# An adaptive-norm feed-forward kernel: a second home for x, one group turned instead of summed on TensorE, another load order, and a wait for GpSimd

## The chip, the cores and the metric

The kernel runs on one core of a Trainium2 chip. The metric is the device time of one execution in microseconds (us); lower is better. Each time given for a kernel is the median of several executions.

## The reference

x has 32 batches of 64 rows of 512 values, cond 32 rows of 256. In float32:

```
q_emb = relu(cond @ W3 + b3)                       # (32, 512)
x1    = (64 * x + sum of x over the 64 rows) * q_emb[:, None, :]
h0    = relu(x1 @ W2 + b2)                         # (32, 64, 512)
w1    = ternary(W_fc)                              # (2048, 512)
y     = square(relu(h0 @ w1.T))                    # (32, 64, 2048)
yn    = y * rsqrt(mean(y * y, last) + 2**-23)
out   = x + yn @ ternary(W_proj).T                 # W_proj (512, 2048)
```

ternary(w) takes groups of 64 weights; scale is the mean of their absolute values, and each weight becomes -scale, 0 or +scale (round and clip of w / scale, in bfloat16).

## The kernel before

The 2048 rows of x make 4 groups of 512 rows (8 batches each), a group 4 tiles of 128 rows (t). The hidden size 2048 makes 16 tiles (j) of 128.

**Stage one, 16 units** (unit u: group g = u // 4, column block m = u % 4). For a group, sum_x multiplies every 128x128 block of x by the constant matrix sum_mat (64 times the row itself plus the batch's sum, so it transposes x and does the sum in the same product) into PSUM ps_out[:, k]; for each of the 4 blocks k, DVE's scale_x multiplies by q_t from PSUM into x1_t[:, g % 2, k] (a ring of two groups). make_h0(u) then is 4 float32 products of 128x512. ACT's relu_h0(u) applies bias and relu into h0_f (ring of 2), DVE's round_h0(u) rounds to h0_hi, and GpSimd's rest_of_h0(u) subtracts to get h0_lo (both float32r parts that TensorE multiplies in one pass each). sum_x(0) stands before unit 0, sum_x(g + 1) before unit 4g + 2 (SUMS_AT = 2). Three PSUM buffers (ACC_RING) hold products, so unit u waits for relu_h0(u - 3).

**Weights, 16 pairs, beside it.** A pair is 128 x 1024 weights. SyncE's queue loads it (load_pair, three raw buffers), ACT takes the absolute value and the sign (read_pair), DVE sums groups of 64 and makes the scale (sum_pair), ACT spreads the scale (spread_pair), DVE makes the ternary weights with three tensor_tensor operations (ternary_pair), SyncE's queue transposes by DMA (turn_pair), ACT copies into w_t (keep_pair). step(i) of ACT is keep(i - 2), read(i + 2), spread(i + 1); step(i) of DVE is sum(i + 1), ternary(i). STEP_AT_UNIT and STEP_AT_TILE say at which unit or tile each step stands; every engine works strictly in the order written:

```
STEP_AT_UNIT = {0: 0, 1: 1, 3: 2, 4: 3, 5: 4, 7: 5, 8: 6, 9: 7, 11: 8, 12: 9, 13: 10, 15: 11}
STEP_AT_TILE = {1: 12, 3: 13, 5: 14, 7: 15}
```

In DVE's loop over units, unit u is: round_h0(u - 1), then at u % 4 == 2 the four scale_x of the next group, then its step. In ACT's loop it is relu_h0(u - 1), then its step.

**Stage two, 64 tiles** (tile v: group v // 16, hidden tile j = v % 16). hidden(v) is 8 float32r products into ps_acc, ACT takes relu, square (y) and square again (y_sq, ring of 2), DVE's split_y(v) makes y_hi (cast) and y_lo (subtraction), project(v) is 8 products into ps_out. TensorE's order is hidden(v + 2), project(v). add_squares(v) adds y_sq into sq_acc on GpSimd (the last one on DVE); at the end of a group DVE's sum_parts reduces it, one small product finishes the sum, inverse_root and finish scale ps_out, add x and store.

**SyncE's queue** issues all loads of x, W2 (load_wv) and the pairs in one written order, with waits in it. x of every group goes to one buffer x_sb, so load_x(g) waits until all of group g - 1 has been summed (xt_done); what stands behind it in the queue waits as well. At the end x_sb takes x again for the residual (load_res).

Of the kernel before, what the change touches and what calls it, by code (L numbers as in the profile page):

```python
# [12 lines left out]
P = 128  # L13
# [15 lines left out]
def wait(engine, semaphore, count):  # L29
    if count > 0:  # L30
        engine.wait_ge(semaphore, count)


def adaln_ffn(
# [44 lines left out]
    SUMS_AT = 2  # L79
    STEP_AT_UNIT = {0: 0, 1: 1, 3: 2, 4: 3, 5: 4, 7: 5, 8: 6, 9: 7, 11: 8, 12: 9, 13: 10, 15: 11}  # L80
    STEP_AT_TILE = {1: 12, 3: 13, 5: 14, 7: 15}
    KEEP_AT_TILE = {8: 14, 9: 15}

    x_rows = x.rearrange("b n d -> (b n) d").rearrange("(g t p) d -> g p t d", p=P, t=TT)
    out_rows = out.rearrange("b n d -> (b n) d").rearrange("(g t p) d -> g t p d", p=P, t=TT)

    with ExitStack() as ctx:
        def sb(name, shape, dt):
            return ctx.enter_context(nc.sbuf_tensor(name, shape, dt))
# [4 lines left out]
        def sem(name):  # L94
            return ctx.enter_context(nc.semaphore(name))
# [18 lines left out]
        sum_mat = sb("sum_mat", [P, P], F32)  # L114
        ident_f = sb("ident_f", [P, P], F32)
# [24 lines left out]
        ps_out = psum("ps_out", [P, TT, BANK], F32)  # L140
# [13 lines left out]
        x_loaded = sem("x_loaded")  # L154
# [28 lines left out]
        split = sem("split")  # L183
# [30 lines left out]
        def _(sp):  # L214
            def load_pair(i):
                wait(sp, sign_ready, i - RAW_RING + 1)
                sp.dma_start(raw[:, i % RAW_RING, :].rearrange("p (i w) -> p i w", i=2), PAIRS[i][0]
                             ).then_inc(raw_loaded[i % RAW_RING], 16)

            def turn_pair(i):  # L220
                sp.wait_ge(tern_ready, i + 1)
                wait(sp, wt_ready, i)
                sp.dma_start_transpose(out=w_turned[:], in_=w_tern[:, i % RING, :]).then_inc(turned, 16)

            def load_wv(i):
                cols = slice(i * P, (i + 1) * P)
                sp.dma_start(wv_sb[:, :, cols], w_v[:, cols].rearrange("(k p) d -> p k d", p=P)
                             ).then_inc(wv_loaded[i], 16)

            def load_x(g):  # L230
                sp.wait_ge(xt_done, KD * g)
                sp.dma_start(x_sb[:], x_rows[g]).then_inc(x_loaded, 16)
# [12 lines left out]
            load_pair(0)  # L245
            load_wv(1)
            load_pair(1)
            load_wv(2)
            load_x(1)
            load_wv(3)  # L250
            load_pair(2)
            load_pair(3)
            for i in range(len(PAIRS)):
                if i + RAW_RING + 1 < len(PAIRS):
                    load_pair(i + RAW_RING + 1)
                turn_pair(i)
                if i == 1:
                    load_x(2)
                if i == 4:
# [12 lines left out]
        def _(pe):  # L272
            def sum_x_block(t, k):
                return pe.matmul(ps_out[:, k, t * P:(t + 1) * P], x_sb[:, t, k * P:(k + 1) * P], sum_mat[:],  # L274
                                 start=True, stop=True)

            def sum_x(g):
                pe.wait_ge(x_loaded, 16 * g)
                pe.wait_ge(x1_ready, KD * g)
                for k in range(KD):  # L280
                    for t in range(TT):
                        last = sum_x_block(t, k)
                    last.then_inc(xt_done, 1)
# [88 lines left out]
            for t in range(TT):  # L372
                if t == TT // 2:
                    pe.wait_ge(condt_ready, 1)
                    pe.wait_ge(wq_loaded, 16)
                    for m in range(KD):
                        for k in range(KQ):
                            last = pe.matmul(ps_x[:, m * BATCHES:(m + 1) * BATCHES], wq_sb[:, k, m * P:(m + 1) * P],  # L378
                                             cond_t[:, k, :], start=(k == 0), stop=(k == KQ - 1))
                    last.then_inc(q_done, 1)  # L380
                pe.wait_ge(x0_loaded[t], 16)
                for k in range(KD):
                    last = sum_x_block(t, k)
                    if t == TT - 1:
                        last.then_inc(xt_done, 1)

            for u in range(UNITS):
                if u % KD == SUMS_AT and u // KD + 1 < GROUPS:
                    sum_x(u // KD + 1)
                make_h0(u)  # L390
            for v in range(AHEAD):
                hidden(v)
# [13 lines left out]
        def _(dve):  # L406
# [29 lines left out]
            def scale_x(g, k):  # L436
                dve.wait_ge(xt_done, KD * g + k + 1)
                wait(dve, h0_done, KD * (g - 1))
                x1 = x1_t[:, g % RING, k, :].rearrange("p (b n) -> p b n", n=N)
                dve.tensor_tensor(x1, ps_out[:, k, :].rearrange("p (b n) -> p b n", n=N),  # L440
                                  q_t[:, k, g * GB:(g + 1) * GB].rearrange("p (b o) -> p b o", o=1).to_broadcast([P, GB, N]),
                                  ALU.mult).then_inc(x1_ready, 1)

# [164 lines left out]
        def _(pool):  # L608
# [56 lines left out]
```

## Time and profile before

| | |
|---|---|
| median of 3 runs | 318.5 us (317.95 to 319.53) |
| the profiled execution's own time | 317.89 us |
| its span, first to last instruction | 315.8 us |
| busy: TensorE, DVE, ACT, GpSimd | 310.0, 210.4, 192.1, 110.8 us |
| moved by DMA | 27.02 MB, mean 86 GB/s |

The span is a little shorter than the execution's time, which also holds what lies around the instructions. Busy time is the sum of what an engine's instructions took. In the rows, PE is TensorE's product, ACT is ScalarE, DVE is VectorE, POOL is GpSimd, SPq is SyncE's queue. L293 is line 293 of the kernel. Merged rows have a count (x16); float32 products leave two records each.

### The profile page before, as it was taken

The page shows a single profiled execution, that of the slowest core. Times are in us where ns is not written, and L with a number is a line of the kernel's source. Part 1 is how long each engine was busy: PE and PEld are TensorE (multiplying, and loading weights), DVE is VectorE, ACT ScalarE, POOL GpSimd, SP SyncE. Part 2 cuts the span into 40 slices and gives each one's busy share as a digit, 9 for nine tenths or more (in the row PEclk, how much of TensorE's full clock was granted, in tenths as well). Part 3 has the DMA queues.
Part 4 walks back from the last instruction along what each step waited for, and adds up shares of the span by engine and source line. Part 5 has one row for each costly group of instructions (what it writes and reads, how often), then busy time and mean ns, then how long its engine had stood idle before and what let it go on. Part 6 is the DMA issues. An engine that isn't in the chain of part 4 may idle for free.

```text
span 315.8 us, 3835 instructions
## 1 busy us (share of the span) xinstructions
PE 310.0 (98%) x1326; PEld 237.8 (75%) x1326; DVE 210.4 (67%) x290; ACT 192.1 (61%) x282; POOL 110.8 (35%) x94
## 2 busy tenths in 40 slices
PE   8999999999999999999999999999999999999995
PEld 7664645545887788888888888888888888888884
DVE  0639989798888856677556665856665676665555
ACT  1668987899996886445554444654445554445550
POOL 1004333233743535414334441334443314443330
PEclk9999999999999999999999999999999999999999
DMA  6994959489521110007000000510000024000003
GB/s 183 361 287 122 282 136 296 103 198 265 87 50 34 33 36 1 0 13 254 0 0 2 0 0 0 209 61 0 0 2 0 0 105 162 0 0 2 0 1 134
DMA packets 31331, 27.02 MB, mean 86 GB/s; under 512 B 18736, under 2 KB 20816, under 8 KB 31312
## 3 DMA queue, kind: packets, MB, share of 16 engines
q1 hardware_dynamic: 29984, 26.25, 29.0%
q10 hardware_dynamic: 1328, 0.53, 0.7%
q8 instruction: 10, 0.16, 0.2%
q14 instruction: 9, 0.07, 0.1%
HBM read 18.39 MB, written 4.19 MB: 71 GB/s over the span
## 4 chain that ended last, share of the span: by engine, by line
PE 90%; ACT 4%; issue 3%; DVE 2%; POOL 0%; POOLq 0%; DVEq 0%; ACTq 0%
PE ps_out L321 34%; PE ps_acc L309 32%; PE ps_acc L293 17%; PE ps_out L274 4%; ACT x_t L569 1%; ACT x_t L566 1%; PE ps_acc L363 1%; DVE abs_sum L413 1%; DVE y_hi L453 1%; PE ps_x L378 1%; PE ps_acc L370 0%; ACT w_scale L533 0%; ACT w_t L546 0%; ACT w_abs L527 0%; PE ps_x L353 0%
## 5 line engine op out<-in xcount | busy, mean ns | idle before, releaser
L211 POOL TENSOR_TENSOR wv_sb<-wv_sb 128x512 f32<-128x512 f32 x55 | 80.0, 1454 | 113.6 <-ACT wv_sb L572 113.6
L321 PE MATMUL ps_out<-w_t,y_hi 128*128 128x512 f32 x256 | 100.2, 392 | 0.4 <-DVE y_lo L455 0.4
L309 PE MATMUL ps_acc<-h_hi,w_t 128*128 128x512 f32 x256 | 100.0, 391 | 0.0
L321 PE MATMUL ps_out<-w_t,y_lo 128*128 128x512 f32 x256 | 99.7, 389 | 0.0
L309 PE MATMUL ps_acc<-h_lo,w_t 128*128 128x512 f32 x256 | 99.6, 389 | 0.0
L455 DVE TENSOR_TENSOR y_lo<-x_t,y_hi 128x512 fp32r<-128x512 f32 x64 | 91.3, 1426 | 2.2
L566 ACT ACTIVATE x_t<-ps_acc 128x512 f32<-128x512 f32 x64 | 38.0, 594 | 78.5 <-PE ps_acc L309 78.4
L453 DVE CAST y_hi<-x_t 128x512 fp32r<-128x512 f32 x64 | 29.2, 456 | 70.8 <-PE ps_out L321 63.3
L321 PEld LDWEIGHTS ps_out<-w_t,y_hi 128*128 128x128 f32 x256 | 48.1, 188 | 11.1 <-DVE y_lo L455 0.8
L293 PE MATMUL ps_acc<-x_t,wv_sb 128*128 128x512 f32 x128 | 55.7, 593 | 0.3 <-DVE x_t L440 0.3
L309 PEld LDWEIGHTS ps_acc<-h_hi,w_t 128*128 128x128 f32 x256 | 48.1, 188 | 10.2 <-issue 0.2
L309 PEld LDWEIGHTS ps_acc<-h_lo,w_t 128*128 128x128 f32 x256 | 48.1, 188 | 10.2 <-issue 0.2
L321 PEld LDWEIGHTS ps_out<-w_t,y_lo 128*128 128x128 f32 x256 | 48.1, 188 | 9.8
L293 PEld LDWEIGHTS ps_acc<-x_t,wv_sb 128*128 128x128 f32 x128 | 24.0, 190 | 29.1 <-issue 28.4
L569 ACT ACTIVATE x_t<-x_t 128x512 f32<-128x512 f32 x64 | 40.5, 632 | 2.0
L572 ACT ACTIVATE wv_sb<-x_t 128x512 f32<-128x512 f32 x64 | 40.5, 632 | 2.1
L613 POOL TENSOR_TENSOR h_lo<-h_f,h_hi 128x512 fp32r<-128x512 f32 x16 | 20.4, 1272 | 58.4 <-DVE h_hi L447 58.4
L533 ACT ACTIVATE w_scale<-scale 128x1024 bf16<-128x1024 bf16 x16 | 16.8, 1047 | 4.6 <-DVE scale L416 4.6
L413 DVE TENSOR_REDUCE abs_sum<-w_abs 128x16 f32<-128x1024 bf16 x16 | 19.4, 1212 | 0.2 <-ACT w_abs L527 0.2
L527 ACT ACTIVATE w_abs<-raw 128x1024 bf16<-128x1024 f32 x16 | 16.7, 1046 | 4.1 <-DMA raw<-in_L_ffn_W_proj_dram 2.9
L528 ACT ACTIVATE w_sign<-raw 128x1024 bf16<-128x1024 f32 x16 | 16.7, 1043 | 0.0
L274 PEld LDWEIGHTS ps_out<-sum_mat,x_sb 128*128 128x128 f32 x128 | 15.4, 197 | 1.4 <-issue 1.2
(49 smaller groups left out, 147.1 us busy)
## 6 DMA issues: line engine op xcount, KB each, us to landing
x_sb<-in_x_dram SPq DMA_DIRECT2D x7, 1024.0 KB, 6.0
raw<-in_L_ffn_W_fc_dram SPq DMA_DIRECT2D x8, 512.0 KB, 5.6
raw<-in_L_ffn_W_proj_dram SPq DMA_DIRECT2D x8, 512.0 KB, 6.2
out_dram<-x_t SPq DMA_DIRECT2D x16, 256.0 KB, 2.1
x_sb<-in_x_dram SPq DMA_DIRECT2D x4, 256.0 KB, 5.5
wv_sb<-in_L_cond_W_dram SPq DMA_DIRECT2D x4, 256.0 KB, 7.3
x_t<-in_L_cond_W_dram ACTq DMA_DIRECT2D x1, 512.0 KB, 4.6
w_turned<-w_tern SPq DMA_TRANSPOSE x16, 3.1
```

The lines of the kernel that those rows point to most:

```text
L211: engine.tensor_tensor(sq_acc[:], sq_acc[:], y_sq[:, v % SQ_RING, :], ALU.add).then_inc(sq_added, 1)
L274: return pe.matmul(ps_out[:, k, t * P:(t + 1) * P], x_sb[:, t, k * P:(k + 1) * P], sum_mat[:], start=True, stop=True)
L293: last = pe.matmul(ps_acc[:, u % ACC_RING, :], wv_sb[:, k, m * P:(m + 1) * P], x1_t[:, g % RING, k, :], start=(k == 0), stop=(k == KD - 1))
L309: last = pe.matmul(ps_acc[:, (UNITS + v) % ACC_RING, :], w_t[:, j, k * P:(k + 1) * P], part[:, k, g * BANK:(g + 1) * BANK], start=(k == 0 ...
L321: last = pe.matmul(ps_out[:, t, :], part[:, v % RING, t * P:(t + 1) * P], w, start=(j == 0 and part is y_hi), stop=(j == HJ - 1 and part i ...
L413: dve.tensor_reduce(abs_sum[:], grouped(w_abs[:, i % READ_RING, :]), AX.X, ALU.add).then_inc(sum_ready, 1)
L453: dve.tensor_copy(y_hi[:, v % RING, :], y[:, v % RING, :]).then_inc(hi_done, 1)
L455: dve.tensor_tensor(y_lo[:, v % RING, :], y[:, v % RING, :], y_hi[:, v % RING, :], ALU.subtract).then_inc(split, 1)
L566: act.activation(relu_y[:, v % RING, :], ps_acc[:, (UNITS + v) % ACC_RING, :], ACT.Relu).then_inc(relued, 1)
L569: act.activation(y[:, v % RING, :], relu_y[:, v % RING, :], ACT.Square).then_inc(y_ready, 1)
L572: act.activation(y_sq[:, v % SQ_RING, :], y[:, v % RING, :], ACT.Square).then_inc(sq_ready, 1)
L613: pool.tensor_tensor(h0_lo[:, m, cols], h0_f[:, u % RING, :], h0_hi[:, m, cols], ALU.subtract).then_inc(h0_split, 1)
```

## The change

1. A second buffer x_odd takes x of groups 1 and 3 (it shares its place with y_hi and y_lo, which are first used in stage two). load_x(g) now waits for the sums of group g - 2.
2. In SyncE's order pair 2 stands before load_x(1), load_wv(3) after; load_x(2) and load_x(3) stand one pair earlier (after turn_pair(0) and turn_pair(3)).
3. x of group 3 is not multiplied by sum_mat: turn_x(3, k) transposes its blocks with the identity (k = 0 before unit 8, k = 1 before unit 9, k = 2 and 3 before unit 10), and DVE's scale_x(3, k), at the same units, does the rest in three operations, each waiting for the one before: a sum over the 64 rows, 64 times x plus the sum, and the product with q_t.
4. GpSimd's add_squares(v), for v up to 61, waits for split_y(v).

```
--- before.py
+++ after.py
@@ -79,6 +79,12 @@
     SUMS_AT = 2
     STEP_AT_UNIT = {0: 0, 1: 1, 3: 2, 4: 3, 5: 4, 7: 5, 8: 6, 9: 7, 11: 8, 12: 9, 13: 10, 15: 11}
     STEP_AT_TILE = {1: 12, 3: 13, 5: 14, 7: 15}
+
+    SUMS_OF_UNIT = [[0], [1], [2, 3], []]
+
+    def sums_by_vector(g):
+        return g == GROUPS - 1
+
     KEEP_AT_TILE = {8: 14, 9: 15}
 
     x_rows = x.rearrange("b n d -> (b n) d").rearrange("(g t p) d -> g p t d", p=P, t=TT)
@@ -102,6 +108,9 @@
         x1_t = sb("x1_t", [P, RING, KD, BANK], F32)
         x_sb = sb("x_sb", [P, TT, D], F32)
         wv_sb = sb("wv_sb", [P, KD, D], F32)
+
+        with nc.sbuf_tensor("x_odd", [P, TT, D], F32) as x_odd:
+            pass
         y_hi = sb("y_hi", [P, RING, BANK], F32R)
         y_lo = sb("y_lo", [P, RING, BANK], F32R)
         raw = sb("raw", [P, RAW_RING, 2 * BANK], F32)
@@ -122,9 +131,11 @@
         mean_sq = sb("mean_sq", [P, TT], F32)
         root = sb("root", [P, TT], F32)
         rstd = sb("rstd", [P, TT], F32)
+        batch_sum = sb("batch_sum", [P, GB], F32)
         wq_sb = x1_t[:, 1, 0:KQ, :]
         cond_sb = h0_f[0:BATCHES, 0, 0:Q]
         cond_t = h0_f[:, 1, 0:KQ * BATCHES].rearrange("p (k b) -> p k b", k=KQ)
+        x_of = [x_sb, x_odd]
         x_res = x_sb
         rstd0 = h0_f[:, 0, 0:TT]
         rsq = h0_f[:, 0, TT:2 * TT]
@@ -151,7 +162,7 @@
         bias_loaded = sem("bias_loaded")
         wv_loaded = [sem(f"wv_loaded{i}") for i in range(KD)]
         x0_loaded = [sem(f"x0_loaded{t}") for t in range(TT)]
-        x_loaded = sem("x_loaded")
+        x_loaded = [sem(f"x_loaded{i}") for i in range(2)]
         res_loaded = sem("res_loaded")
         raw_loaded = [sem(f"raw_loaded{i}") for i in range(RAW_RING)]
         condt_done = sem("condt_done")
@@ -159,6 +170,7 @@
         q_done = sem("q_done")
         q_ready = sem("q_ready")
         xt_done = sem("xt_done")
+        summed = sem("summed")
         x1_ready = sem("x1_ready")
         h0_done = sem("h0_done")
         h0_relued = sem("h0_relued")
@@ -228,8 +240,8 @@
                              ).then_inc(wv_loaded[i], 16)
 
             def load_x(g):
-                sp.wait_ge(xt_done, KD * g)
-                sp.dma_start(x_sb[:], x_rows[g]).then_inc(x_loaded, 16)
+                wait(sp, xt_done, KD * (g - 1))
+                sp.dma_start(x_of[g % 2][:], x_rows[g]).then_inc(x_loaded[g % 2], 16)
 
             def load_res(g):
                 if g == 0:
@@ -246,17 +258,17 @@
             load_wv(1)
             load_pair(1)
             load_wv(2)
+            load_pair(2)
             load_x(1)
             load_wv(3)
-            load_pair(2)
             load_pair(3)
             for i in range(len(PAIRS)):
                 if i + RAW_RING + 1 < len(PAIRS):
                     load_pair(i + RAW_RING + 1)
                 turn_pair(i)
-                if i == 1:
+                if i == 0:
                     load_x(2)
-                if i == 4:
+                if i == 3:
                     load_x(3)
                 if i == 9:
                     load_res(0)
@@ -270,17 +282,25 @@
 
         @block.tensor
         def _(pe):
-            def sum_x_block(t, k):
-                return pe.matmul(ps_out[:, k, t * P:(t + 1) * P], x_sb[:, t, k * P:(k + 1) * P], sum_mat[:],
+            def sum_x_block(g, t, k):
+                return pe.matmul(ps_out[:, k, t * P:(t + 1) * P], x_of[g % 2][:, t, k * P:(k + 1) * P], sum_mat[:],
                                  start=True, stop=True)
 
             def sum_x(g):
-                pe.wait_ge(x_loaded, 16 * g)
+                pe.wait_ge(x_loaded[g % 2], 16 * ((g + 1) // 2))
                 pe.wait_ge(x1_ready, KD * g)
                 for k in range(KD):
                     for t in range(TT):
-                        last = sum_x_block(t, k)
+                        last = sum_x_block(g, t, k)
                     last.then_inc(xt_done, 1)
+
+            def turn_x(g, k):
+                pe.wait_ge(x_loaded[g % 2], 16 * ((g + 1) // 2))
+
+                pe.wait_ge(x1_ready, KD * (g - 1) + k + 1)
+                for t in range(TT):
+                    last = pe.transpose(ps_out[:, k, t * P:(t + 1) * P], x_of[g % 2][:, t, k * P:(k + 1) * P], ident_f[:])
+                last.then_inc(xt_done, 1)
 
             def make_h0(u):
                 g, m = u // KD, u % KD
@@ -380,13 +400,17 @@
                     last.then_inc(q_done, 1)
                 pe.wait_ge(x0_loaded[t], 16)
                 for k in range(KD):
-                    last = sum_x_block(t, k)
+                    last = sum_x_block(0, t, k)
                     if t == TT - 1:
                         last.then_inc(xt_done, 1)
 
             for u in range(UNITS):
-                if u % KD == SUMS_AT and u // KD + 1 < GROUPS:
-                    sum_x(u // KD + 1)
+                after = u // KD + 1
+                if after < GROUPS and sums_by_vector(after):
+                    for k in SUMS_OF_UNIT[u % KD]:
+                        turn_x(after, k)
+                elif after < GROUPS and u % KD == SUMS_AT:
+                    sum_x(after)
                 make_h0(u)
             for v in range(AHEAD):
                 hidden(v)
@@ -437,7 +461,18 @@
                 dve.wait_ge(xt_done, KD * g + k + 1)
                 wait(dve, h0_done, KD * (g - 1))
                 x1 = x1_t[:, g % RING, k, :].rearrange("p (b n) -> p b n", n=N)
-                dve.tensor_tensor(x1, ps_out[:, k, :].rearrange("p (b n) -> p b n", n=N),
+                src = ps_out[:, k, :].rearrange("p (b n) -> p b n", n=N)
+                if g > 0 and sums_by_vector(g):
+                    at = 2 * (KD * [v for v in range(1, GROUPS) if sums_by_vector(v)].index(g) + k)
+                    wait(dve, summed, at)
+                    dve.tensor_reduce(batch_sum[:], src, AX.X, ALU.add).then_inc(summed, 1)
+                    dve.wait_ge(summed, at + 1)
+                    dve.scalar_tensor_tensor(out=x1, in0=src, scalar=float(N),
+                                             in1=batch_sum[:].rearrange("p (b o) -> p b o", o=1).to_broadcast([P, GB, N]),
+                                             op0=ALU.mult, op1=ALU.add).then_inc(summed, 1)
+                    dve.wait_ge(summed, at + 2)
+                    src = x1
+                dve.tensor_tensor(x1, src,
                                   q_t[:, k, g * GB:(g + 1) * GB].rearrange("p (b o) -> p b o", o=1).to_broadcast([P, GB, N]),
                                   ALU.mult).then_inc(x1_ready, 1)
 
@@ -499,7 +534,10 @@
                 g, m = u // KD, u % KD
                 if u > 0:
                     round_h0(u - 1)
-                if g + 1 < GROUPS and m == SUMS_AT:
+                if g + 1 < GROUPS and sums_by_vector(g + 1):
+                    for k in SUMS_OF_UNIT[m]:
+                        scale_x(g + 1, k)
+                elif g + 1 < GROUPS and m == SUMS_AT:
                     for k in range(KD):
                         scale_x(g + 1, k)
                 if u in STEP_AT_UNIT:
@@ -636,6 +674,9 @@
                                    base=QUAD * (r + 1) - P, pattern=[[-1, P]], channel_multiplier=1).then_inc(quad_made, 1)
             for v in range(TILES - 1):
                 if v % HJ > 0:
+
+                    if v < TILES - 2:
+                        pool.wait_ge(split, v + 1)
                     add_squares(pool, v)
```

## Rows read from the trace of the kernel before

**Rows 1.** The page: busy time of each engine; the granted TensorE clock in 40 slices.
```profile
PE 310.0 (98%) x1326; PEld 237.8 (75%) x1326; DVE 210.4 (67%) x290; ACT 192.1 (61%) x282; POOL 110.8 (35%) x94
...
PEclk9999999999999999999999999999999999999999
```

**Rows 2.** The chain that ended last, up to 120 us: start, us, what.
```profile
4.03 0.35 PE ps_acc L366 x2
...
7.69 1.71 PE ps_x L378 x16
...
53.26 3.57 PE ps_out L274 x32
56.84 20.60 PE ps_acc L293 x48
```

**Rows 3.** The same chain, 130 to 145 us.
```profile
136.43 1.81 PE ps_acc L309 x8
```

**Rows 4.** Timeline of TensorE: start, us, line, operation; the first projection.
```profile
82.76 0.39 PE L321 MATMUL ps_out<-w_t,y_hi 128*128 128x512 f32 x1
```

**Rows 5.** Timeline of ACT; in brackets idle time before, and releaser.
```profile
19.42 1.06 ACT L527 ACTIVATE w_abs<-raw 128x1024 bf16<-128x1024 f32 x1 [2.85 <-DMA raw<-in_L_ffn_W_proj_dram]
...
43.00 0.69 ACT L561 ACTIVATE h_f<-ps_acc,bv_t 128x512 f32<-128x512 f32 x1 [0.72 <-PE ps_acc L293]
...
63.74 1.04 ACT L533 ACTIVATE w_scale<-scale 128x1024 bf16<-128x1024 bf16 x1
...
78.54 0.67 ACT L561 ACTIVATE h_f<-ps_acc,bv_t 128x512 f32<-128x512 f32 x1
79.32 0.60 ACT L566 ACTIVATE x_t<-ps_acc 128x512 f32<-128x512 f32 x1
...
82.98 1.05 ACT L546 ACTIVATE w_t<-w_turned 128x1024 fp32r<-128x1024 bf16 x1
...
90.40 1.05 ACT L546 ACTIVATE w_t<-w_turned 128x1024 fp32r<-128x1024 bf16 x1
...
101.76 1.05 ACT L533 ACTIVATE w_scale<-scale 128x1024 bf16<-128x1024 bf16 x1 [2.34 <-DVE scale L416]
```

**Rows 6.** Groups by line and form, DVE: count, busy, mean ns, idle before.
```profile
L413 DVE TENSOR_REDUCE abs_sum<-w_abs 128x16 f32<-128x1024 bf16 x16 | 19.4, 1212 | 0.2 <-ACT w_abs L527 0.2
...
L489 DVE SCALAR_TENSOR_TENSOR x_t<-ps_out,rstd,x_sb 128x512 f32<-128x512 f32 x16 | 11.0, 746 | 0.3
...
L440 DVE TENSOR_TENSOR x_t<-ps_out,q_t 128x512 f32<-128x512 f32 x16 | 9.9, 682 | 6.1 <-PE ps_out L274 6.1
```

**Rows 7.** Timeline of DVE, 58 to 101 us.
```profile
58.96 0.43 DVE L447 CAST h_hi<-h_f 128x512 fp32r<-128x512 f32 x1 [2.21 <-ACT h_f L561]
59.30 2.48 DVE L440 TENSOR_TENSOR x_t<-ps_out,q_t 128x512 f32<-128x512 f32 x4
...
62.03 1.21 DVE L413 TENSOR_REDUCE abs_sum<-w_abs 128x16 f32<-128x1024 bf16 x1
63.27 0.22 DVE L416 TENSOR_SCALAR scale<-abs_sum 128x16 bf16<-128x16 f32 x1
...
65.46 0.42 DVE L447 CAST h_hi<-h_f 128x512 fp32r<-128x512 f32 x1
...
81.61 0.69 DVE L455 TENSOR_TENSOR y_lo<-x_t,y_hi 128x512 fp32r<-128x512 f32 x1
...
98.65 1.74 DVE L455 TENSOR_TENSOR y_lo<-x_t,y_hi 128x512 fp32r<-128x512 f32 x1
```

**Rows 8.** Timeline of GpSimd.
```profile
59.46 1.27 POOL L613 TENSOR_TENSOR h_lo<-h_f,h_hi 128x512 fp32r<-128x512 f32 x1 [4.79 <-DVE h_hi L447]
...
98.55 1.29 POOL L211 TENSOR_TENSOR wv_sb<-wv_sb 128x512 f32<-128x512 f32 x1 [0.22 <-ACT wv_sb L572]
```

**Rows 9.** Timeline of SyncE's queue: the fourth transpose.
```profile
38.94 1.24 SPq L223 DMA_TRANSPOSE w_turned<-w_tern  x1
```

**Rows 10.** The page, DMA issues: count, KB each, median us to landing.
```profile
x_sb<-in_x_dram SPq DMA_DIRECT2D x7, 1024.0 KB, 6.0
```

More of the change, by code:

```diff
@@ L81, in adaln_ffn, with sums_by_vector @@
     STEP_AT_TILE = {1: 12, 3: 13, 5: 14, 7: 15}
+    SUMS_OF_UNIT = [[0], [1], [2, 3], []]
+    def sums_by_vector(g):
+        return g == GROUPS - 1
     KEEP_AT_TILE = {8: 14, 9: 15}
@@ L104, in adaln_ffn @@
         wv_sb = sb("wv_sb", [P, KD, D], F32)
+        with nc.sbuf_tensor("x_odd", [P, TT, D], F32) as x_odd:
+            pass
         y_hi = sb("y_hi", [P, RING, BANK], F32R)
@@ L124, in adaln_ffn @@
         rstd = sb("rstd", [P, TT], F32)
+        batch_sum = sb("batch_sum", [P, GB], F32)
         wq_sb = x1_t[:, 1, 0:KQ, :]
@@ L127, in adaln_ffn @@
         cond_t = h0_f[:, 1, 0:KQ * BATCHES].rearrange("p (k b) -> p k b", k=KQ)
+        x_of = [x_sb, x_odd]
         x_res = x_sb
@@ L153, in adaln_ffn @@
         x0_loaded = [sem(f"x0_loaded{t}") for t in range(TT)]
-        x_loaded = sem("x_loaded")
+        x_loaded = [sem(f"x_loaded{i}") for i in range(2)]
         res_loaded = sem("res_loaded")
@@ L161, in adaln_ffn @@
         xt_done = sem("xt_done")
+        summed = sem("summed")
         x1_ready = sem("x1_ready")
@@ L230, in load_x @@
             def load_x(g):
-                sp.wait_ge(xt_done, KD * g)
-                sp.dma_start(x_sb[:], x_rows[g]).then_inc(x_loaded, 16)
+                wait(sp, xt_done, KD * (g - 1))
+                sp.dma_start(x_of[g % 2][:], x_rows[g]).then_inc(x_loaded[g % 2], 16)
             def load_res(g):
@@ L248, in _ @@
             load_wv(2)
+            load_pair(2)
             load_x(1)
             load_wv(3)
-            load_pair(2)
             load_pair(3)
@@ L256, in _ @@
                 turn_pair(i)
-                if i == 1:
+                if i == 0:
                     load_x(2)
-                if i == 4:
+                if i == 3:
                     load_x(3)
@@ L272, in _, with sum_x_block @@
         def _(pe):
-            def sum_x_block(t, k):
-                return pe.matmul(ps_out[:, k, t * P:(t + 1) * P], x_sb[:, t, k * P:(k + 1) * P], sum_mat[:],
+            def sum_x_block(g, t, k):
+                return pe.matmul(ps_out[:, k, t * P:(t + 1) * P], x_of[g % 2][:, t, k * P:(k + 1) * P], sum_mat[:],
                                  start=True, stop=True)
             def sum_x(g):
-                pe.wait_ge(x_loaded, 16 * g)
+                pe.wait_ge(x_loaded[g % 2], 16 * ((g + 1) // 2))
                 pe.wait_ge(x1_ready, KD * g)
@@ L281, in sum_x, with turn_x @@
                     for t in range(TT):
-                        last = sum_x_block(t, k)
+                        last = sum_x_block(g, t, k)
                     last.then_inc(xt_done, 1)
+            def turn_x(g, k):
+                pe.wait_ge(x_loaded[g % 2], 16 * ((g + 1) // 2))
+                pe.wait_ge(x1_ready, KD * (g - 1) + k + 1)
+                for t in range(TT):
+                    last = pe.transpose(ps_out[:, k, t * P:(t + 1) * P], x_of[g % 2][:, t, k * P:(k + 1) * P], ident_f[:])
+                last.then_inc(xt_done, 1)
             def make_h0(u):
@@ L382, in _ @@
                 for k in range(KD):
-                    last = sum_x_block(t, k)
+                    last = sum_x_block(0, t, k)
                     if t == TT - 1:
@@ L387, in _ @@
             for u in range(UNITS):
-                if u % KD == SUMS_AT and u // KD + 1 < GROUPS:
-                    sum_x(u // KD + 1)
+                after = u // KD + 1
+                if after < GROUPS and sums_by_vector(after):
+                    for k in SUMS_OF_UNIT[u % KD]:
+                        turn_x(after, k)
+                elif after < GROUPS and u % KD == SUMS_AT:
+                    sum_x(after)
                 make_h0(u)
@@ L439, in scale_x @@
                 x1 = x1_t[:, g % RING, k, :].rearrange("p (b n) -> p b n", n=N)
-                dve.tensor_tensor(x1, ps_out[:, k, :].rearrange("p (b n) -> p b n", n=N),
+                src = ps_out[:, k, :].rearrange("p (b n) -> p b n", n=N)
+                if g > 0 and sums_by_vector(g):
+                    at = 2 * (KD * [v for v in range(1, GROUPS) if sums_by_vector(v)].index(g) + k)
+                    wait(dve, summed, at)
+                    dve.tensor_reduce(batch_sum[:], src, AX.X, ALU.add).then_inc(summed, 1)
+                    dve.wait_ge(summed, at + 1)
+                    dve.scalar_tensor_tensor(out=x1, in0=src, scalar=float(N),
+                                             in1=batch_sum[:].rearrange("p (b o) -> p b o", o=1).to_broadcast([P, GB, N]),
+                                             op0=ALU.mult, op1=ALU.add).then_inc(summed, 1)
+                    dve.wait_ge(summed, at + 2)
+                    src = x1
+                dve.tensor_tensor(x1, src,
                                   q_t[:, k, g * GB:(g + 1) * GB].rearrange("p (b o) -> p b o", o=1).to_broadcast([P, GB, N]),
@@ L501, in _ @@
                     round_h0(u - 1)
-                if g + 1 < GROUPS and m == SUMS_AT:
+                if g + 1 < GROUPS and sums_by_vector(g + 1):
+                    for k in SUMS_OF_UNIT[m]:
+                        scale_x(g + 1, k)
+                elif g + 1 < GROUPS and m == SUMS_AT:
                     for k in range(KD):
@@ L638, in _ @@
                 if v % HJ > 0:
+                    if v < TILES - 2:
+                        pool.wait_ge(split, v + 1)
                     add_squares(pool, v)
```

## The prediction

> **What bounds the kernel now.** I read the page first [rows 1]: TensorE is busy 98% of the span at the upper of its two clock levels (granted clock 1.00 in every slice). So time can only leave by taking work from TensorE or closing its few gaps, and can enter through anything that lets it wait. Then the chain that ended last [rows 2, 3]: almost all TensorE, except between 79 and 105 us, where it runs over ACT and DVE. That is the place to look at, since TensorE there is busy too and only just so.
>
> The first stage (unit u takes 20.60 / 6 = 3.43 us) runs beside the preparation of 16 weight pairs, which ACT and DVE do in their program order between the units' relus and casts. Going backwards in ACT's timeline [rows 5]: from the spread at 63.74 (pair 9) to relu_h0(15) at 78.54, ACT is back to back; that is 14.80 us that only its own queue sets. After relu_h0(15) come hidden tile 0, its split on DVE (y_lo 81.61 + 0.69 = 82.30 [rows 7]) and the first projection at 82.76 [rows 4]. The spare time there is only 0.46 us. Going further, one hidden and one projected tile take 2 x 1.81 us [rows 3]: from 82.76, 15 of each would end at 82.76 + 54.39 = 137.15; they end at 136.43 + 1.81 = 138.24. So TensorE loses 1.09 us there, in small waits for split. The reason: two tiles and one weight step take ACT 90.40 - 82.98 = 7.42 us [rows 5], TensorE 7.25, but the round over DVE is longer: y_lo takes 1.74 instead of 0.69 us whenever GpSimd's add of squares runs beside it (98.65 beside 98.55 [rows 7, 8]), and the sum of the next pair, which ACT's spread waits for (idle 2.34 at 101.76 [rows 5]), is queued behind it.
>
> **TensorE's part.** Group 3's sums are 32 passes in 3.57 us [rows 2]. A float32 product is two passes here; a transpose leaves one record each (two transposes, x2, 0.35 us [rows 2]), so 16 remain. Passes with only 32 moving columns but a full 128x128 load took 1.71 / 16 = 0.107 us [rows 2], against 3.57 / 32 = 0.112 with 128 columns: the load sets the pitch. So 16 x 0.112 = 1.79 us, saving 1.78. Bounds: 0 saved if a transpose costs two passes; 2.66 if it goes like the 128 columns of a one-pass product (1.81 / 8 / 4 = 0.057 us). I take 1.78; below, this choice turns out to be covered by a wait. (The Trainium skill, "TensorE: Matmul & The Clock Gate", Part 4: PE-mode transpose, gives about 275 ns for a 128x128 bf16 transpose inside a kernel. By it 16 would cost 4.4 us and the part would lose 0.8 us; no row of a 128x128 transpose decides this.)
>
> **DVE's part.** For each k of group 3 one tensor_tensor (0.60 of the queue: the four at 59.30 take 2.48, of which the last 0.08 overlaps what follows [rows 7]) becomes three dependent operations. Reduce of 512 from PSUM: the reduce of 1024 takes 1.21 [rows 6]; if nearly all scales with columns it is 0.6, with a fixed part like the others' I take 0.70. Scalar_tensor_tensor from PSUM: 0.75 [rows 6]. The product, now with two SBUF inputs, at the 0.69 of y_lo [rows 7], of which 0.08 overlaps the next. With two steps of 0.03 over a semaphore, c = 0.70 + 0.03 + 0.75 + 0.03 + 0.61 = 2.12 us. Bounds: 1.8 (three times 0.60) and 2.64 (the reduce at its full 1.21). Extra: 4 x (2.12 - 0.60) = 6.1 us.
>
> Now the queue. The early gains of the new load order (pair 2 lands while ACT is still at pair 1, so the idle 2.85 at 19.42 goes) cannot outlive 43.00, where ACT waits for TensorE's unit 6 anyway [rows 5]: 53.26 - 3 x 3.43 = 42.97 [rows 2], unchanged. From there ACT does relu 0.57 and four operations of 0.95 (four such and a relu of 0.57 fill each unit of the full queue; (78.54 - 63.74 - 4 x 0.57) / 13 = 0.96 [rows 5]), so relu_h0(7) starts at 47.37, ends at 48.05, DVE rounds from 48.09. From here DVE never waits until it has pair 9's scale: 4 rounds x 0.34 (58.96 to 59.30), 4 x 2.12, the remaining steps of pairs 7 and 8 at 65.46 - 62.03 = 3.43 each, and sum and scale of pair 9, 1.24 + 0.22 [rows 7]: 1.36 + 8.48 + 6.86 + 1.46 = 18.16, so 66.25. Before, this scale ended at 63.27 + 0.22 = 63.49 and ACT took it at 63.74, its own queue being later. Of the extra 6.1 us the idle 2.21 at 58.96 [rows 7] and the earlier start take about 3.3. **ACT's spread of pair 9 comes at 66.3, 2.5 us late**, and ACT has no gap until relu_h0(15): 78.54 + 2.5 = 81.1. Hidden tile 0 started 79.32, after a wait for TensorE; now at 81.1 + 0.57 = 81.6, 2.3 late. Split 0 ends 82.30 + 2.3 = 84.6, the first projection starts 84.65 in place of 82.76: **+1.9 us**. TensorE, with 1.78 us less work, could have been there at 80.98: it waits 3.7 us in all, before hidden(0), hidden(2) and the projection. So the saved passes are worth nothing here, whether 0 or 2.66. Restarting on a just-arrived split costs another **+0.1**.
>
> Group 3's x1 itself is ready at 48.09 + 4 x 0.34 + 4 x 2.12 + 2 x 3.43 - 0.34 = 64.5 or so; unit 12 starts at 56.84 + 2 x 3.43 - 1.78 = 61.9 and wants block k = 3 at 64.5: no more than a touch.
>
> **GpSimd's wait.** Behind the waiting add only later adds are queued; ACT's square of tile v + 2 and DVE's sum_parts wait for it. It starts some 1 us later than now (the cast and y_lo of its tile), while sum_parts has a whole stretch of 1.81 more before TensorE wants it: nothing. y_lo falls from 1.74 to 0.69 where it met the add: 1.05 us off the round that makes TensorE wait, in two of the last rounds; ACT's 7.42 against TensorE's 7.25 remains for one of them. I give back nearly all of the 1.09: **-1.0**. (The Trainium skill, "SBUF — State Buffer", Who interferes with whom: a DVE instruction with two SBUF inputs blocks against a GpSimd one that reads SBUF, and so does a cast in its two-port mode. The first half agrees with 1.74 against 0.69. The second speaks against this edit: the add is moved beside the next tile's cast. By it a cast would lose up to 0.3 us and the gain would be 0.7 to 0.8.) The product in c starts 1.83 us after its round; GpSimd's subtraction ends 0.50 + 1.27 = 1.77 after it [rows 7, 8]: just clear, and if not, the upper c covers it.
>
> **x's second home and the loads.** load_x(3) now stands behind the fourth transpose, issued at 38.94 + 1.24 = 40.2 at the latest [rows 9]; landing 6.0 later [rows 10] it is there by 46.2, and turn_x(3, 0) wants it at 46.4. With the earlier pairs it is some 2 us sooner. Were it 1 us late, unit 8 would slip, but DVE needs k = 0 only at 48.4: below 2 us late, nothing. The first transfers only queue sooner behind the same bytes: nothing before 43.00.
>
> **Sum:** +1.9 + 0.1 - 1.0 = +1.0 us on the profiled execution's 317.89 (span 315.8), 318.9. The runs' median lies 0.6 above that execution, so 319.5.
>
> **Rivals.**
> (a) *TensorE alone decides; faster.* If DVE's added work disappears in its waits, the first projection comes 1.78 sooner and the 1.09 go: -2.9, 315.6. For it: TensorE's 98%, DVE's 67% average. Against: DVE's idle in that stretch is 2.2 us, not 6. The point from which it decides: each 0.1 of c moves the first projection by 0.4 us, so no change needs c = 1.87, and faster by over 0.5% (1.6 us) c below 1.5, less than three operations of 0.60 can give. Only an overlap that I don't see (or ACT's queue being shorter than its rows) helps. 0.15.
> (b) *The lag is larger or nothing is paid back; slower.* c = 2.64 adds 4 x 0.52 = 2.1: 321.6. No payback, because the add now meets the next cast and the weight step's two-input products: +2.0, 320.5. Together 0.28.
> (c) *x(3) late* by over 2 us through the crowding of 3 MB of queued transfers: each us beyond is one more in DVE's full queue; at 3 late, 320.5. 0.04.
> (d) *The wait for split does nothing and c is at its lower bound:* 319.5 - 1.3 + 1.0 = 319.2; it falls in with the forecast.
>
> **How the numbers follow.** Forecast case (0.53): c between 1.8 and 2.3 with payback, -0.3 to +1.7 us, 318.2 to 320.2. Half a per cent is 1.6 us, about what a measurement can tell from no change. Faster 0.15 is (a); slower 0.30 is (b), part of (c); the rest is same, 0.55. The range runs from 316.3 (part of (a)) to 321.6 (the upper c).
>
> **What would show it.** In the profile after: spread of pair 9 near 66.3; the first projection near 84.6 with TensorE idle 3 to 4 us between 75 and 85; group 3's turning passes 16 at 0.11; reduce, scalar_tensor_tensor and product at 0.70, 0.75, 0.69; y_lo's mean falling from 1.43 to 0.7; no wait after 90 us. I am wrong if DVE waits between 48 and 66, or TensorE does not between 75 and 85.

## The result, and the profile after

| | before | after |
|---|---|---|
| median of 12 runs each, us | 318.18 | 319.05 |
| ratio, 95% interval | | 1.0022 (1.0013 to 1.0031) |
| profiled execution, us | 317.89 | 318.91 |
| its span, us | 315.8 | 317.1 |

The change makes the kernel 0.22% slower: 0.7 us by the ratio (0.4 to 1.0), 0.87 us between the medians. That is a real difference, under the half per cent that was taken as the bound of "same". The forecast was 319.5 (range 316.3 to 321.6). On the profiled executions it was +1.0 us, and they differ by 1.02; their spans differ by 1.3.

TensorE after the change, the rows that answer to [rows 2, 4]: the first unit, the turning passes and the three places where it waits.

```profile
11.77 7.11 PE L313 MATMUL ps_acc<-x_t,wv_sb 128*128 128x512 f32 x16 [0.28 <-DVE x_t L475]
...
46.45 0.60 PE L302 MATMUL ps_out<-ident_f,x_odd 128*128 128x128 f32 x4
...
50.33 0.60 PE L302 MATMUL ps_out<-ident_f,x_odd 128*128 128x128 f32 x4
...
54.20 1.04 PE L302 MATMUL ps_out<-ident_f,x_odd 128*128 128x128 f32 x8
...
76.51 0.50 PE L329 MATMUL ps_acc<-h_hi,w_t 128*128 128x512 f32 x1 [0.65 <-ACT h_f L599]
...
81.70 0.50 PE L329 MATMUL ps_acc<-h_hi,w_t 128*128 128x512 f32 x1 [1.26 <-ACT h_f L599]
...
84.89 0.47 PE L341 MATMUL ps_out<-w_t,y_hi 128*128 128x512 f32 x1 [1.08 <-DVE y_lo L490]
```

The 4 transposes of k = 0 begin at 46.45 and the next unit's product at 46.89: 0.11 us each, and one record each, where a float32 product leaves two. TensorE then waits for nothing until 76.51. There it waits for relu_h0(13), which frees a PSUM buffer; at 81.70 it waits for relu_h0(15), at 84.89 for the split of tile 0. The first projection was at 82.76 [rows 4]. The first unit of the kernel before began 0.22 us sooner than the 11.77 here:

```profile
11.55 7.11 PE L293 MATMUL ps_acc<-x_t,wv_sb 128*128 128x512 f32 x16 [0.28 <-DVE x_t L440]
```

ACT, answering to [rows 5]:

```profile
43.22 0.69 ACT L599 ACTIVATE h_f<-ps_acc,bv_t 128x512 f32<-128x512 f32 x1 [3.55 <-PE ps_acc L313]
...
66.11 1.05 ACT L571 ACTIVATE w_scale<-scale 128x1024 bf16<-128x1024 bf16 x1 [3.15 <-DVE scale L440]
...
80.98 0.67 ACT L599 ACTIVATE h_f<-ps_acc,bv_t 128x512 f32<-128x512 f32 x1
81.55 0.59 ACT L604 ACTIVATE x_t<-ps_acc 128x512 f32<-128x512 f32 x1
...
102.63 1.06 ACT L571 ACTIVATE w_scale<-scale 128x1024 bf16<-128x1024 bf16 x1 [1.57 <-DVE scale L440]
```

The spread of pair 9 is at 66.11 after 3.15 us of waiting for DVE's scale, where it was 63.74; relu_h0(15) is at 80.98 (78.54), hidden tile 0 at 81.55 (79.32). At 102.63 ACT still waits for the last scale, 1.57 us where it was 2.34.

DVE, answering to [rows 7]: one turned block of group 3 (48.64 to 50.70), the scale of pair 9, a cast and a y_lo of the weight steps in stage two.

```profile
48.30 0.43 DVE L482 CAST h_hi<-h_f 128x512 fp32r<-128x512 f32 x1 [0.51 <-ACT h_f L599]
48.64 0.68 DVE L468 TENSOR_REDUCE batch_sum<-ps_out 128x8 f32<-128x512 f32 x1
49.36 0.69 DVE L470 SCALAR_TENSOR_TENSOR x_t<-ps_out,batch_sum 128x512 f32<-128x512 f32 x1
50.09 0.69 DVE L475 TENSOR_TENSOR x_t<-x_t,q_t 128x512 f32<-128x512 f32 x1
50.70 1.21 DVE L437 TENSOR_REDUCE abs_sum<-w_abs 128x16 f32<-128x1024 bf16 x1
...
65.86 0.21 DVE L440 TENSOR_SCALAR scale<-abs_sum 128x16 bf16<-128x16 f32 x1
...
82.84 1.18 DVE L488 CAST y_hi<-x_t 128x512 fp32r<-128x512 f32 x1 [0.47 <-ACT x_t L607]
...
99.48 1.00 DVE L488 CAST y_hi<-x_t 128x512 fp32r<-128x512 f32 x1 [0.67 <-ACT x_t L607]
100.51 0.69 DVE L490 TENSOR_TENSOR y_lo<-x_t,y_hi 128x512 fp32r<-128x512 f32 x1
```

GpSimd beside it, answering to [rows 8]:

```profile
82.44 1.29 POOL L651 TENSOR_TENSOR h_lo<-h_f,h_hi 128x512 fp32r<-128x512 f32 x1 [2.49 <-DVE h_hi L482]
...
98.89 1.30 POOL L223 TENSOR_TENSOR wv_sb<-wv_sb 128x512 f32<-128x512 f32 x1 [3.70 <-DVE y_lo L490]
101.28 1.29 POOL L223 TENSOR_TENSOR wv_sb<-wv_sb 128x512 f32<-128x512 f32 x1 [1.09 <-DVE y_lo L490]
```

Two more rows by line and form, y_lo (L490) and the turning (L302), and the row of the chain that ended last which closes the stretch of [rows 3]:

```profile
L490 DVE TENSOR_TENSOR y_lo<-x_t,y_hi 128x512 fp32r<-128x512 f32 x64 | 47.2, 738 | 2.2
...
L302 PE MATMUL ps_out<-ident_f,x_odd 128*128 128x128 f32 x16 | 2.2, 272 | 0.0
```

```profile
139.54 0.13 PE ps_x L379 x2
```

y_lo has a mean of 0.74 us; it was 1.43. From the first projection at 84.89, 15 hidden and 15 projected tiles would end at 84.89 + 54.39 = 139.28; they end at 139.54. So 0.26 us are lost where 1.09 were.

Two figures of each trace will serve for the comparisons below. The lead is the time from the start of the first unit to the first projection: 82.76 - 11.55 = 71.21 us before, 84.89 - 11.77 = 73.12 after. The loss is what 15 hidden and 15 projected tiles take beyond 54.39: 1.09 and 0.26.

### The profile page after: what moved, and what is told of

The parts are those of the page before. It is cut to its first block, busy times and chain, and to the rows that moved or that the text cites. A ratio compares the mean times of both kernels' runs of the same rounds, so it can differ in the third digit from the quotient of the medians.

```text
span 317.1 us, 3817 instructions
## 1 busy us (share of the span) xinstructions
PE 308.7 (97%) x1310; PEld 235.6 (74%) x1310; DVE 173.6 (55%) x298; ACT 191.6 (60%) x282; POOL 102.7 (32%) x94
## 4 chain that ended last, share of the span: by engine, by line
PE 85%; DVE 6%; ACT 4%; issue 3%; DMA 1%; POOL 0%; DVEq 0%; POOLq 0%; ACTq 0%; SPq 0%
PE ps_out L341 37%; PE ps_acc L329 35%; PE ps_acc L313 8%; PE ps_out L286 3%; DVE abs_sum L437 2%; DMA w_turned<-w_tern 1%; ACT w_abs L565 1%; ACT h_f L599 1%; PE ps_acc L383 1%; ACT w_scale L571 1%; DVE x_t L470 1%; DVE batch_sum L468 1%; PE ps_x L398 1%; ACT w_t L584 0%; DVE w_abs L450 0%
## 5 line engine op out<-in xcount | busy, mean ns | idle before, releaser
L223 POOL TENSOR_TENSOR wv_sb<-wv_sb 128x512 f32<-128x512 f32 x55 | 71.4, 1298 | 115.1 <-DVE y_lo L490 111.3
L488 DVE CAST y_hi<-x_t 128x512 fp32r<-128x512 f32 x64 | 30.4, 475 | 107.0 <-PE ps_out L341 99.0
L490 DVE TENSOR_TENSOR y_lo<-x_t,y_hi 128x512 fp32r<-128x512 f32 x64 | 47.2, 738 | 2.2
L219 POOL TENSOR_TENSOR wv_sb<-wv_sb 128x512 f32<-128x512 f32 x4 | 6.2, 1554 | 26.1 <-DVE y_lo L490 26.1
```

Source lines behind the costliest of these rows:

```text
L488: dve.tensor_copy(y_hi[:, v % RING, :], y[:, v % RING, :]).then_inc(hi_done, 1)
L490: dve.tensor_tensor(y_lo[:, v % RING, :], y[:, v % RING, :], y_hi[:, v % RING, :], ALU.subtract).then_inc(split, 1)
```

## The experiments

Ratios are to the kernel before, run on the same chip; 1 in the third decimal is 0.32 us.

| | what | median, us | ratio, 95% interval |
|---|---|---|---|
| after | the change | 319.05 | 1.0022 (1.0013 to 1.0031) |
| e1 | no turning | 317.36 | 0.9966 (0.9953 to 0.9980) |
| e2 | no wait for the split | 320.31 | 1.0059 (1.0046 to 1.0072) |
| e3 | before, with only the wait for the split | 317.36 | 0.9975 (0.9963 to 0.9986) |
| e4 | turning without the sum | 315.57 | 0.9913 (0.9900 to 0.9926) |
| e5 | each block turned twice | 319.41 | 1.0031 (1.0019 to 1.0042) |
| e6 | group 2 turned in place of 3 | 317.86 | 0.9984 (0.9974 to 0.9993) |
| e7 | group 3's product on GpSimd | 317.40 | 0.9967 (0.9955 to 0.9979) |
| e8 | group 2 turned, its product on GpSimd | 315.23 | 0.9901 (0.9885 to 0.9917) |
| e9 | before, with only the loads and x's second home | 318.44 | 0.9997 (0.9989 to 1.0006) |
| e10 | e8 with x(1) loaded later | 315.55 | 0.9905 (0.9890 to 0.9920) |

**e1, no turning.**

```
     def sums_by_vector(g):
-        return g == GROUPS - 1
+        return False
```

> The changed kernel with group 3 summed on TensorE again (32 passes, one DVE operation per block), everything else of the change kept. My theory (DVE's added 5.8 us make ACT late by 2.4 us and TensorE waits some 4 us before the first projection): the lag goes, TensorE's 1.78 us come back, the wait for the split still pays 0.8 to 1.0: 317.2 to 317.6, faster than before by 0.6 to 1.0 us, first projection near 83.0. Rival (the turning was a gain and another part, the loads or the wait for the split, cost more than that): this kernel is slower than the changed one, over 319.5.

317.36, near the middle of what my theory gave. So the turning costs 0.56% (1.8 us) beside the rest of the change, and the rest is worth about 1 us. The first projection is at 83.55 and not near 83.0, but the first unit of this execution began at 12.35: the lead is 71.20, as before the change, and the loss 0.17.

**e2, no wait for the split.**

```
                 if v % HJ > 0:
-                    if v < TILES - 2:
-                        pool.wait_ge(split, v + 1)
                     add_squares(pool, v)
```

> The changed kernel without GpSimd's wait for the split. My theory: y_lo is back at 1.4 us mean, the round over DVE in the weight steps is again longer than TensorE's 7.25 us per two tiles, so 0.8 to 1.1 us come on top: 320.0. Rival (the wait has no effect on the time, or costs some by its collision with the next cast): 319.0 or less.

320.31. TensorE's timeline: the first projection, and a later one that waits for the split once more. Below it the same wait in the kernel before, and the row of the chain that ends the stretch here.

```profile
85.07 0.47 PE L341 MATMUL ps_out<-w_t,y_hi 128*128 128x512 f32 x1 [1.08 <-DVE y_lo L490]
...
107.59 0.50 PE L341 MATMUL ps_out<-w_t,y_hi 128*128 128x512 f32 x1 [0.35 <-DVE y_lo L490]
```

```profile
105.20 0.50 PE L321 MATMUL ps_out<-w_t,y_hi 128*128 128x512 f32 x1 [0.35 <-DVE y_lo L455]
```

```profile
140.62 0.13 PE ps_x L379 x2
```

140.62 - 85.07 - 54.39 = 1.16 us lost there, near the 1.09 before the change. So GpSimd's wait is worth 0.9 us in the traces and 1.2 us (0.37%) in the times.

**e3, the wait for the split alone.** The same two lines of e2, put into the kernel before.

> The kernel before with nothing but GpSimd's wait for the split. My theory: 0.8 to 1.0 us faster than before, 317.3, with no TensorE gap at 105 us. Rival (the loads were what paid back): same as before, 318.2.

0.25% faster, 0.8 us (0.4 to 1.2), with no TensorE wait in that stretch of the trace. First projection, and the end of the stretch in the chain:

```profile
82.85 0.39 PE L321 MATMUL ps_out<-w_t,y_hi 128*128 128x512 f32 x1
```

```profile
137.42 0.13 PE ps_x L359 x2
```

137.42 - 82.85 - 54.39 = 0.18 us lost, 0.91 less than before. The loads are not needed for this part.

**e4, turning without the sum.** This kernel leaves out the sum over the rows for group 3.

```
-                if g > 0 and sums_by_vector(g):
-                    at = 2 * (...)
-                    wait(dve, summed, at)
-                    dve.tensor_reduce(batch_sum[:], src, AX.X, ALU.add).then_inc(summed, 1)
-                    dve.wait_ge(summed, at + 1)
-                    dve.scalar_tensor_tensor(out=x1, in0=src, scalar=float(N), ...).then_inc(summed, 1)
-                    dve.wait_ge(summed, at + 2)
-                    src = x1
```

> The changed kernel with the sum over the rows and its addition left out for group 3, so x of that group is only turned and multiplied by q_t (this leaves out part of the computation). DVE's work is as before, TensorE's is 1.78 us less. My theory: nothing makes ACT late, the first projection comes near 81.2, the whole saving and the split wait's show: 315.4 to 315.8. Rival (the turning itself or its place before units 8 to 10 disturbs TensorE, or something other than DVE delays ACT): 317 or more.

315.57. TensorE's first projection:

```profile
81.34 0.39 PE L341 MATMUL ps_out<-w_t,y_hi 128*128 128x512 f32 x1
```

3.5 us sooner than after the change, with the same turning on TensorE and no wait between 12 us and there; the lead is 69.38, 1.83 below the kernel before. The product with q_t is still there; it reads PSUM again, at 0.68 us where it took 0.69. So DVE's two added operations a block are the difference between 319.05 and 315.57.

**e5, each block turned twice.**

```
-                for t in range(TT):
-                    last = pe.transpose(...)
+                for twice in range(2):
+                    for t in range(TT):
+                        last = pe.transpose(...)
```

> The changed kernel with each block of group 3 turned twice (32 transposes in place of 16, the same result), 1.78 us more work for TensorE before units 8 to 10. My theory (TensorE has 4 us to spare before the first projection, so what its passes cost there is worth nothing): as the changed kernel, 319.1, within 0.3. Rival (TensorE's own work counts there too): 320.8.

319.41 against 319.05; the ratios differ by 0.09%, less than their intervals. TensorE: one block's turning, now 8 passes, and the waits.

```profile
47.00 1.04 PE L303 MATMUL ps_out<-ident_f,x_odd 128*128 128x128 f32 x8
...
82.25 0.50 PE L330 MATMUL ps_acc<-h_hi,w_t 128*128 128x512 f32 x1 [0.44 <-ACT h_f L600]
...
85.44 0.47 PE L342 MATMUL ps_out<-w_t,y_hi 128*128 128x512 f32 x1 [1.08 <-DVE y_lo L491]
```

1.78 us more work, yet the first projection starts only 85.44 - 84.89 = 0.55 us later, and 0.54 of that is there at the first unit already (12.31 against 11.77 us, see e9). The lead is 73.13 against 73.12. TensorE's wait before hidden(0) is gone in exchange, and the one before hidden(2) fell from 1.26 to 0.44.

**e6, group 2 in place of group 3.**

```
-        return g == GROUPS - 1
+        return g == GROUPS - 2
```

> The changed kernel with group 2 turned before units 4, 5 and 6 instead of group 3; group 3 summed on TensorE. DVE's extra 5.8 us fall where ACT later waits 3.5 us for TensorE anyway (the wait before relu_h0(6)). My theory: ACT is some 2 us late at 49 us but catches up by relu_h0(10); first projection near 82, 316.1 to 316.9, faster than e1 (317.36). Rival (DVE's extra work costs the same wherever it stands): 319.

317.86: better than group 3, but no better than e1, and 1 us above the range that I expected; the theory missed. ACT:

```profile
48.88 1.05 ACT L571 ACTIVATE w_scale<-scale 128x1024 bf16<-128x1024 bf16 x1 [3.15 <-DVE scale L440]
...
55.78 1.06 ACT L579 ACTIVATE w_t<-w_turned 128x1024 fp32r<-128x1024 bf16 x1 [0.92 <-DMA w_turned<-w_tern]
...
64.84 1.05 ACT L571 ACTIVATE w_scale<-scale 128x1024 bf16<-128x1024 bf16 x1 [1.18 <-DVE scale L440]
```

DVE, when it gets relu_h0(9):

```profile
60.28 0.43 DVE L482 CAST h_hi<-h_f 128x512 fp32r<-128x512 f32 x1 [1.53 <-ACT h_f L599]
```

The lag of 2 us at 48.88 (46.88 before) is what I had put in. It is not made up. ACT's copy at 55.78 waits 0.92 us for the weights' transposing DMA, which was issued at 51.52, when ACT's copy before it had ended at 51.45. So ACT comes late with relu_h0(9), DVE starts group 3's products 1.3 us later than before the change (60.28 against 58.96), and ACT waits for DVE's scale again at 64.84, 1.1 us later than the 63.74 before. I had added up ACT's queue alone; the lag goes round ACT, the DMA and DVE. The lead is 71.79.

**e7, group 3's product on GpSimd.** DVE's scale_x of group 3 ends after its second operation; GpSimd does the third.

```
+            def scale_turned(k):
+                x1 = x1_t[:, 3 % RING, k, :].rearrange("p (b n) -> p b n", n=N)
+                pool.wait_ge(summed, 2 * (k + 1))
+                pool.tensor_tensor(x1, x1, <q_t of group 3, broadcast>, ALU.mult).then_inc(x1_ready, 1)
             for u in range(UNITS):
                 rest_of_h0(u)
+                for k in <blocks that DVE sums in unit u + 1>:
+                    scale_turned(k)
```

> The changed kernel with group 3's third operation (product with q_t) on GpSimd behind its h0 subtraction, so DVE's cost of a block falls from 2.06 to 1.43 us. My theory: each us off DVE between 48 and 66 is one off ACT's lag (4 x 0.63 = 2.5), so the lag of 2.4 is gone, the first projection comes near 82.4, 316.6 to 317.0. Rival (GpSimd's reads block DVE's two-input operations, or GpSimd's own queue is late for unit 12): 318 or more.

317.40, over the 316.6 to 317.0 of the theory. Each block gave 0.6 to 0.7 us back on DVE, but one operation grew. DVE's scale of pair 9, and GpSimd's product and the subtraction beside it:

```profile
63.41 0.99 DVE L440 TENSOR_SCALAR scale<-abs_sum 128x16 bf16<-128x16 f32 x1
```

```profile
60.44 1.04 POOL L669 TENSOR_TENSOR x_t<-x_t,q_t 128x512 f32<-128x512 f32 x1
...
63.10 1.26 POOL L651 TENSOR_TENSOR h_lo<-h_f,h_hi 128x512 fp32r<-128x512 f32 x1
```

The scale is a 128x16 operation of 0.22 us; here it takes 0.99, until about when GpSimd's subtraction ends (63.10 + 1.26 = 64.36). These 0.77 us are of the size that the run missed of its forecast (0.4 to 0.8); no run without them shows it. Of the turning's saving on TensorE nothing is left: the lead is 71.22.

**e8, group 2 turned, its product on GpSimd.** e6 and e7 together.

> Group 2 turned, with its product on GpSimd. My theory: no lag is left at relu_h0(10), TensorE's 1.78 us show in full beside the split wait's 0.9: 315.4 to 315.8, as e4 (315.57). Rival: no better than e6.

315.23, as said: 1% faster than the kernel before, 3.8 us faster than after. Three places where ACT waits, between 41 and 59 us:

```profile
41.42 0.69 ACT L599 ACTIVATE h_f<-ps_acc,bv_t 128x512 f32<-128x512 f32 x1 [0.62 <-PE ps_acc L313]
...
46.91 1.06 ACT L571 ACTIVATE w_scale<-scale 128x1024 bf16<-128x1024 bf16 x1 [1.97 <-DVE scale L440]
...
58.72 0.69 ACT L599 ACTIVATE h_f<-ps_acc,bv_t 128x512 f32<-128x512 f32 x1 [1.47 <-PE ps_acc L313]
```

```profile
81.17 0.39 PE L341 MATMUL ps_out<-w_t,y_hi 128*128 128x512 f32 x1
```

At 41.42 and 58.72 ACT waits for TensorE again, so no lag is carried past them; the one wait for a scale between them (46.91, with the same 0.99 us operation in it) is absorbed. The first projection is at 81.17; 82.76 - 1.78 + 0.23, by which the first unit began later, is 81.21.

**e9, the loads alone, and e10, x(1) later.** In e9 no group is turned and GpSimd doesn't wait for the split; e10 is e8 with one line:

```
             load_pair(2)
+            sp.wait_ge(xt_done, KD)
             load_x(1)
```

> The kernel before with only x's second home and the new order of the loads (no turning, no wait for the split). In the traces so far the first unit of stage one began at 11.77 to 12.35 us with the new order and at 11.55 and 11.63 with the old one. Theory A (the earlier x(1) and pair 2 take DMA time from the first tiles of x or W3, on which the first unit waits): 0.2 to 0.6 us slower than before, 318.5 to 318.9, first unit near 12, and the early pair 2 gives nothing back. Theory B (as in my prediction: the loads change nothing): 318.3, within 0.15 of before.

> e8 (group 2 turned, product on GpSimd) with the wait for the sums of group 0 put ahead of load_x(1) again, pair 2 kept early. Theory A: the first unit begins at 11.6 in place of 11.8 or later, 0.2 us off e8's 315.23: 315.0. Theory B: as e8. If x(1) now lands after 18.6, TensorE waits for it and the time is over 315.4.

e9 is the same as before (0.9997), though its profiled execution began its first unit latest of all:

```profile
12.45 7.10 PE L313 MATMUL ps_acc<-x_t,wv_sb 128*128 128x512 f32 x16 [0.28 <-DVE x_t L475]
```

e10 is as e8, within the intervals, and TensorE doesn't wait for x(1) in it. Its trace names what held up its first unit: the second tile of group 0's x, whose DMA took 5.38 us from 1.67 on.

```profile
7.09 1.16 PE L287 MATMUL ps_out<-sum_mat,x_sb 128*128 128x128 f32 x8 [0.74 <-DMA x_sb<-in_x_dram]
```

Over 12 traces the first unit begins between 11.55 and 12.45 us. The two with the old order are the earliest (11.55 and 11.63), the ten with the new one lie from 11.77 up, which looks like theory A. The other executions speak against it: the spans of e9's 12 run from 316.0 to 316.8 us (median 316.4), those of the 17 executions of the kernel before beside it from 316.0 to 317.4 (median 316.3), and the trace of e9 is of one of the longest of its 12, at 316.8, while the trace of the kernel before, at 315.8, is among the shortest of its kernel. So the start varies from one execution to the next in either order; a mean cost of the new order of up to 0.2 us isn't excluded (interval 0.9989 to 1.0006). The before and after executions shown here differ by 0.22 us in it.

## Why the prediction was right

**TensorE's part.** 16 passes at 0.11, saving 1.78: as put. That the saving is worth nothing here was shown from both sides: 1.78 us added changed nothing clear of the intervals (e5), and with DVE's part gone, or standing elsewhere, it shows in full (leads of 69.38 in e4 and 69.39 in e8 against 71.21). The 275 ns of the Trainium skill ("TensorE: Matmul & The Clock Gate", Part 4: PE-mode transpose) agree with the length of a turning record, 272 ns here; the 4.4 us that the prediction made of them do not come, because the records overlap and the pitch is 0.11.

**DVE's part.** A block costs 50.70 - 48.64 = 2.06 us (put at 2.12: the scalar_tensor_tensor takes 0.69, not 0.75). From DVE's round at 48.30 to the end of pair 9's scale at 66.07 are 17.77 us, where 18.16 were added up. ACT's spread is at 66.11 (66.3), relu_h0(15) at 80.98 (81.1), hidden tile 0 at 81.55 (81.6), the first projection at 84.89 (84.65). All of these hold the 0.22 us of the later first unit, which the forecast did not have. Without it the scale came 0.4 us sooner than put, and 0.22 of that was lost again in tile 0's cast, which took 1.18 us and not 0.96 beside GpSimd's subtraction; the lead grew by 73.12 - 71.21 = 1.91, against +1.9. The mechanism is as put; that its errors cancel to 0.01 is luck. TensorE's 3.7 us of waiting is 84.89 - (82.76 - 1.78 + 0.22) = 3.69; the brackets add up to 2.99, since they begin only when the last record has ended.

**The restart**, put at +0.1: the kernels whose first projection waits lose 0.26 to 0.29 (after, e5, e6, e7), those where it doesn't 0.17 or 0.18 (e1, e3, e4, e8, e10). After the change that is 0.26 - 0.17 = 0.09.

**GpSimd's wait.** Put at -1.0. The 0.26 of the change holds the restart; the wait alone is worth 1.09 - 0.18 = 0.91 in the traces (e3; 0.90 by e2), and 0.8 (0.4 to 1.2) in the times. The slower casts came, as the rule of the Trainium skill ("SBUF — State Buffer", Who interferes with whom) says: 1.00 us at 99.48 beside GpSimd's add at 98.89, where an undisturbed one is 0.43. But TensorE waits nowhere after 84.89, so they cost nothing that the trace shows, and the 0.7 to 0.8 which the prediction gave by that rule is lower than the 0.91; the times alone don't decide between the two.

**The loads** change nothing clear of the interval (e9, with a lead of 71.22 and a loss of 1.11, as before); x(3), issued at 37.62, was there when it was wanted at 46.45.

The sum in the spans: +1.91 (lead) + 0.09 (restart) - 0.92 (GpSimd's wait) + 0.22 (the start) = +1.30, 315.8 to 317.1. The forecast had +1.0 for the first three, which make 1.08. Two things that it did not have nearly cancel in the times of the profiled executions, and that these differ by 1.02 is luck: the 0.22 of the start, and the time outside the span, 2.1 us before and 1.8 after. That second difference is in every kernel here whose DVE does the sums (means of 1.81 to 1.89 us over their executions) and in none of the others (2.01 to 2.04); no run here explains it. The last step, from the profiled execution to the median, was mis-sized: put at 0.6 from three executions, it was 0.29 before and 0.14 after. That is why 319.05 was measured and not 319.5.

Rivals (a), (b), (c) and (d) are out: c was 2.06, GpSimd's wait paid back 0.9, and TensorE did not wait for x(3). What (a) needed can be had, but from another kernel (e8): DVE's work has to stand where ACT afterwards waits for TensorE.

## What to carry to other kernels

In this kernel, with TensorE busy 98% of the time, less work for it was only worth something where its suppliers stayed on time: follow the queues of the engines that feed it, in program order, from the last place where they waited for it to the first where it waits for them. Work added to such a queue costs what it exceeds the idle time up to there, and it costs least just ahead of a wait for the busy engine. A lag can go round several engines and a DMA (e6), so the lag that one queue's sum gives is a lower bound.

## What the runs showed of the hardware

- A DVE operation as small as 128x16 is held up beside GpSimd's two-input operation too: the scale took 0.99 in place of 0.22 us twice (e7, e8) and ended within 0.04 us of GpSimd's subtraction. The 128x512 casts of 1.00 and 1.18 us, in place of 0.43, each ended 0.29 us after GpSimd's operation.
- GpSimd's product with a broadcast operand took 1.04 us for 128x512 in three of four (1.15 in the fourth), its subtraction of two full operands 1.27.
- Issuing a load can hold SyncE's queue for long: pair 2's issue at 6.39, with the first loads still running, took 2.65 us, x(1)'s right behind it, twice as large, 0.47. ACT read pair 2 at 16.45 and TensorE x(1) at 18.71, both without a wait.

```profile
6.39 2.65 SPq L229 DMA_DIRECT2D raw<-in_L_ffn_W_proj_dram  x1
9.08 0.47 SPq L244 DMA_DIRECT2D x_odd<-in_x_dram  x1
...
37.62 0.58 SPq L244 DMA_DIRECT2D x_odd<-in_x_dram  x1
```

What holds the issue up was not tried, nor what makes the start of the first unit vary by up to 0.9 us.
